# Weighted out-degrees summed by TensorE in the preparation, and a plain copy for the eviction of the adjacency bins

## The reference

```python
deg_out = jax.ops.segment_sum(w, s, num_segments=n)   # s: sources and a loop per node
deg_in = jax.ops.segment_sum(w, d, num_segments=n)
inv_sqrt_out = jnp.where(deg_out > 0, jax.lax.rsqrt(deg_out), 0.0)
wn = w * inv_sqrt_out[s] * inv_sqrt_in[d]
def step(h, _):
    agg = jax.ops.segment_sum(h[s] * wn[:, None], d, num_segments=n)
    return ((1.0 - ALPHA) * agg + ALPHA * feat_0, None)
h, _ = jax.lax.scan(step, feat, None, length=K)       # K = 10
```

## Time and profile before

| | before |
|---|---|
| three runs | 4495.53, 4504.68 and 4504.80 us; median 4504.68 us |
| the profiled execution | 4496.91 us, of which its span is 4495.1 us |
| mean granted TensorE clock | 0.867 |
| busy share of the span | PE 70%, PEld 48%, DVE 61%, ACT 21%, POOL 64% |

### The profile page before, as it was taken

How to read it: one execution, slowest core, us unless ns; L and a number is a source line. 1 busy time by engine, 2 the same in 40 slices (tenths; PEclk the granted TensorE clock), 3 DMA queues, 4 the chain that set the end, 5 groups by cost and what they waited for, 6 DMA issues and landing times.

```text
span 4495.1 us, 80143 instructions
## 1 busy us (share of the span) xinstructions
PE 3133.2 (70%) x19503; PEld 2178.5 (48%) x19514; DVE 2732.8 (61%) x9895; ACT 932.9 (21%) x3282; POOL 2884.3 (64%) x3059
## 2 busy tenths in 40 slices
PE   1240117777777999999788875887858778566665
PEld 1240015555554443444366664666646666445554
DVE  6970228777776111111588877888878888765554
ACT  0000003333332000000122221222213222111211
POOL 2677766545556888870277774777747777467776
PEclk9999959989987999999899997999979999755555
DMA  4310024333338999999422223222232222211112
GB/s 143 112 40 10 17 65 88 78 79 81 83 79 217 363 356 362 355 365 354 156 62 62 63 61 51 62 62 62 62 53 62 62 62 62 38 31 28 28 28 30
DMA packets 296107, 497.96 MB, mean 111 GB/s; under 512 B 166411, under 2 KB 211340, under 8 KB 294474
## 3 DMA queue, kind: packets, MB, share of 16 engines
q1 hardware_dynamic: 120919, 340.03, 21.5%
q0 software_dynamic: 92160, 115.39, 14.0%
q10 hardware_dynamic: 82800, 40.01, 3.1%
HBM read 435.66 MB, written 59.08 MB: 110 GB/s over the span
## 4 chain that ended last, share of the span: by engine, by line
PE 30%; POOL 25%; issue 20%; DMA 13%; DVE 9%; DVEq 1%; ACT 1%; SPq 1%; POOLq 0%; another core or an unknown queue 0%; ACTq 0%
PE ps L1571 27%; POOL arena L827 17%; DMA arena<-table,arena 10%; POOL rows_dst L810 7%; DMA rows_dst<-stage,arena 1%; DVE arena L1174 1%; DVE arena L1173 1%; DMA arena<-in_edge_attr_dram 1%; PE ps L1753 1%; DVE arena L1158 1%; DVEq L554 1%; DVE arena L1192 1%; DVE arena L1345 1%; DVE arena L1188 1%; PE ps L1802 1%
## 5 line engine op out<-in xcount | busy, mean ns | idle before, releaser
L827 POOL DMA_INDIRECT arena<-table,arena x2080 | 1981.9, 953 | 1244.2 <-issue 548.8
L1571 PE MATMUL ps<-arena 128*128 128x96 f32 (+4 forms) x8940 | 1485.3, 345 | 616.9 <-DVE arena L1192 255.6
L1571 PEld LDWEIGHTS ps<-arena 128*128 128x128 f32 (+3 forms) x8940 | 1140.4, 217 | 951.4 <-issue 690.2
L1571 PE MATMUL ps<-arena,nodes 125*64 125x500 f32 (+2 forms) x3144 | 649.4, 537 | 32.8 <-DMA arena<-dense 22.3
L1174 DVE TENSOR_SCALAR arena<-iota_row_b,arena 128x128 f32<-128x128 bf16 x2080 | 581.0, 296 | 0.0
L781 POOL DMA_INDIRECT rows_src<-stage,stage_at x400 | 478.0, 1195 | 117.3 <-issue 110.3
L810 POOL DMA_INDIRECT rows_dst<-stage,arena x400 | 393.1, 983 | 229.0 <-issue 124.1
L1186 DVE TENSOR_TENSOR arena<-ps,arena 128x256 f32<-128x256 f32 x416 | 176.3, 424 | 531.2 <-DMA arena<-table,arena 515.8
L1173 DVE TENSOR_SCALAR arena<-iota_row_b,arena 128x128 bf16<-128x128 bf16 x1664 | 456.4, 276 | 2.6 <-PE ps L1571 0.9
L1571 PEld LDWEIGHTS ps<-arena,nodes 125*64 125x64 f32 (+1 forms) x3144 | 242.8, 137 | 351.9 <-issue 319.4
L1277 DVE TENSOR_TENSOR nodes<-nodes,ps 125x256 f32 (+1 forms) x70 | 27.5, 392 | 607.3 <-PE ps L1753 607.3
(11 more groups left out here) (289 smaller groups left out, 3382.2 us busy)
## 6 DMA issues: line engine op xcount, KB each, us to landing
arena<-dense SPq DMA_DIRECT2D x240, 750.0 KB, 7.2
nodes<-dense SPq DMA_DIRECT2D x60, 750.0 KB, 8.2
dense<-arena ACTq DMA_DIRECT2D x150, 250.0 KB
arena<-table,arena POOLq DMA_INDIRECT x2080
arena<-dense SPq DMA_DIRECT2D x60, 500.0 KB, 7.7
arena<-rows_dst SPq DMA_DIRECT2D x208, 96.0 KB
arena<-dense SPq DMA_DIRECT2D x6, 2000.0 KB, 21.2
arena<-pair_rows SPq DMA_DIRECT2D x12, 976.6 KB
```

The lines of the kernel that those rows point to most:

```text
L827: nc.gpsimd.indirect_dma_start(rows[:, u, k, 0:width], None, frm, bass.IndirectOffsetOnAxis(ap=p[:, c, j, c_other:c_other + 1].bitcast(I32 ...
L1571: return nc.tensor.matmul(to, lhsT, rhs, start=start, stop=stop, skip_group_check=True)
```

## The change

The out-degrees no longer come from the eviction. After `place(1, ...)` DVE makes, for each of the 400 tiles of 125 edges, a one-hot of `lo` of the source (`lo_one`, 125 x 128, a ring of `OR = 5`), and for every 50 tiles (`OC = 50`) the product of the one-hot of `hi` with the edge weights (`src_w`, 125 x 50 x 25, two buffers). TensorE adds up 400 matmuls (125 x 128 weights, 25 columns, 32-bit floats) in bank 6, and DVE copies the sum to `deg[:, 0, :]`. All this stands on DVE's list ahead of the first layer norm, and on PE's list behind the look-ups. The eviction of a group becomes one COPY; `deg_parts` and its reduction go. `src_w` and `lo_one` lie on the room of `dst_one`, which is no longer read by then.

```diff
+OC, OR = 50, 5
             place(1, pos_src[:])
+            v.wait_ge(at_loaded, 16 * 2)
+            for c in range(EJ // OC):
+                js = slice(c * OC, (c + 1) * OC)
+                if c >= 2:
+                    v.wait_ge(out_used, OC * (c - 1))
+                link(nc.vector.tensor_tensor(src_w[:, c % 2], src_one[:, js, :], wgt[:, js].unsqueeze(2).to_broadcast([EP, OC, HI]), ALU.mult))
+                for j in range(c * OC, (c + 1) * OC):
+                    if j >= OR:
+                        v.wait_ge(out_used, j - OR + 1)
+                    nc.vector.tensor_scalar(lo_one[:, j % OR, :], iota_row_b[0:EP, :], lo[:, 0, j:j + 1], None, ALU.is_equal).then_inc(out_ready, 1)
+            v.wait_ge(out_summed, 1)
+            link(nc.vector.tensor_copy(deg[:, 0, :], ps[0:LO, 6, 0:HI]))
             v.wait_ge(loaded, 16 * (len(loads) + len(block_loads)))
             layer_norm(link, xs[:], t1[:], t2[:], 0)
...
-            nc.vector.tensor_reduce(deg[:, 0, :], deg_parts[0:LO].rearrange("p d s -> p s d")[:, 0:HI, :], AX_X, ALU.add)
...
-                for r in range(blocks):
-                    ins = nc.scalar.activation(ev[:, slot, r * LO:(r + 1) * LO], ps[:, bank, r * LO:(r + 1) * LO], ACT.Copy,
-                                               accum_out=deg_parts[:, bass.ds(d, 1), g * CB + r])
-                ins.then_inc(ev_ready, 1)
+                nc.scalar.copy(ev[:, slot, 0:blocks * LO], ps[:, bank, 0:blocks * LO]).then_inc(ev_ready, 1)
...
+            for j in range(EJ):
+                pe.wait_ge(out_ready, j + 1)
+                ins = mm(ps[:, 6, 0:HI], lo_one[:, j % OR, :], src_w[:, j // OC % 2, j % OC, :], start=j == 0, stop=j == EJ - 1)
+                ins.then_inc(out_used if j < EJ - 1 else out_summed, 1)
             pe.wait_ge(w3_ready, 1)
```

More of the change, by code:

```diff
@@ L89 @@
 JR = 8
+OC, OR = 50, 5
+assert EJ % OC == 0
 EP_L0, EP_L2, EP_L3 = 0, 1, 1 + LAYERS
@@ L225, in gnn_kernel @@
         used[0] = WORDS - HI * (CG * CB)
-        deg_parts = carve([128, HI, CG * CB])
         used[0] = 0
@@ L290, in gnn_kernel @@
         at16 = carve([EP, EJ, DA])
+        out_from = used[0]
         dst_one = carve([EP, 2, GC, GP], BF16)
+        out_to = used[0]
+        used[0] = out_from
+        src_w = carve([EP, 2, OC, HI])
+        lo_one = carve([EP, OR, 128])
+        assert used[0] <= out_to
+        used[0] = out_to
         assert used[0] <= KEEP_FROM, (used[0], KEEP_FROM)
@@ L503, in gnn_kernel @@
         built = sem("built")
+        out_ready = sem("out_ready")
+        out_used = sem("out_used")
+        out_summed = sem("out_summed")
         bank_free = sem("bank_free")
```

## The result

| | before | changed |
|---|---|---|
| median | 4495.53 us (5 runs) | 4473.67 us (5 runs) |
| ratio to before, 95% interval | 1 | 0.9941, 0.9919 to 0.9962 |
| the same, repeated beside 11 runs of before | 4497.88 us | 4471.67 us; 0.9944, 0.9932 to 0.9957 |
| the profiled execution's span | 4495.1 us | 4462.0 us |

What follows compares the result with a forecast made beforehand. POOL's sends were taken to bound the preparation, TensorE's and DVE's steps each other in the first layer. Terms 4 - 7 - 1.4 = -4.4 us gave 4500.3 us on the level of the runs' median; range 4487 to 4515 us.

Steps and rivals of the forecast that it cites:

- The loop fits: Preparation: the new loop, 0.43 us a matmul, 172 us, hides in DVE's hole before ACT's root; cost 0 us.
- The first rival: Preparation: matmuls do not overlap, the loop takes 320 us and POOL stands still; 4614 us, chance 0.08.
- What the loop does to POOL: Preparation: DVE's eight products lengthen POOL's sends, comparisons add 0; 4 us lost, bounds 0 and 9.
- The second rival: Preparation: comparisons lock the ports shared with POOL, which loses 19 to 38 us; about 4528 us, chance 0.06.
- The eviction: First layer: banks return 0.64 us earlier, shortening TensorE's 19 waits; 7 us gained, bounds 0 and 12.
- The end of the layer: Between the first layer's last matmul and the second layer: the reduction goes, 1.3 us, plus 0.1 of an accumulator read.
- The third rival: First layer: the whole 12 us of bank waits gained, 3 more from ACT's shorter list, POOL unharmed; 4488 us, chance 0.2.

Runs made afterwards that it cites:

- act_copies: Changed kernel with ACT copying the one-hots of `hi` in place of DVE's products, the comparison multiplying by the weight; 0.9925 of the kernel before.
- evict_only: Kernel before with the new plain-copy eviction but not the new loop, out-degrees set to one; 0.9929 of the kernel before.
- unrolled_before: Kernel before with its evictions written out for all 25 d instead of a loop, so no jump back; 0.9971 of the kernel before.
- act_copies_again: act_copies measured again, beside the changed kernel on one chip; 4464.40 us against 4471.67, 0.9927 of the kernel before.
- copy_twice: Changed kernel with each bank copied twice, so that it returns later, with no accumulator; 0.9986 of the kernel before.
- twice_padded: copy_twice with 31 semaphore increments at two places of each d, lengthening ACT's loop body; 1.0012 of the kernel before.

## Why the prediction was wrong, point by point

*The loop fits.* Right in every number: 0.43 us a matmul (0.43 forecast), weight loads of 333 ns (near 324), the request at 485.15 us (485), and ACT's root 25 us behind it. The first rival did not come.

*What the loop does to POOL.* Right in mechanism, too small: 4 us with bounds 0 and 9. Nine of the 147 sends that begin in the stretch last over 1.2 us. Two of them stand beside the layer norm, like both long ones before; the other seven each meet a product. 57 ns more on the mean make 8.4 us. Over all kernels here, the nine with the products start the first layer at 667.9 us on average, the nine without at 659.0. The forecast took the low end of 4 to 7 us because not every product would meet a send at a bad moment; seven of eight did. The second rival, that the comparisons cost as much, falls: the median send beside them takes 959 ns in the changed kernel (958 before), and `act_copies`, which keeps all 400, has a mean of 981 ns.

The Trainium skill, "SBUF — State Buffer", section "Who interferes with whom", says that a DVE instruction with two inputs in SBUF contends with a GpSimd instruction that reads there. By that rule the eight products stretch sends, and the trace agrees with the seven long sends above; that a tensor_scalar holds up a send for its whole length, no send here shows.

*The eviction: the step that failed.* "Where TensorE waited for it, 19 times, that is at most 19 x 0.64 = 12 us" took a label for a count, and made a bound of it. The term was put at 7 us, and measured 33 in the layer of the profile and 32 in the time of `evict_only`. In its place the runs showed three things:

- There were 34 steps that waited for a bank, 36.3 us, of which 21.9 went (37, 38.4 and 23.3 with the gaps that end at other matmuls). The cut itself was well sized: by the timelines the return takes 1.76 us before (772.21 to 773.97 us) and 1.18 after, 0.58 us less against 0.64. With the right count the same product, 34 x 0.64 = 22 us, gives what these gaps lost, in part by luck, since some of it is the jump's.
- ACT's jump, five times 2.6 to 3.1 us before and 0.2 after, was part of it: 3 to 12 us of the layer (10 in `unrolled_before`, of which 7 are gaps at a step). The prediction counted instructions only as durations, never as the length of a loop's body.
- TensorE's matmuls took 11 to 17 us less, with less time at 1.2 GHz. That this follows from the shorter waits, and what of the layer's 33 us it makes, was not shown apart: the four kernels whose layer takes over 730 us are busy 579 to 581 us in it, and most others 555 to 575, but `act_copies_again` has 578 us with 17 gaps.

Late return (18 to 20 us for 0.47 us in `copy_twice`) and jump (12 us from there to `twice_padded`) give the old layer back, so no cost of the accumulators is left over that one profile could tell (some 5 us).

*The end of the layer.* L1225 is gone; its 1.3 us are too few to be seen in these times.

*The rivals and the range.* The third rival (banks worth more, 4488 us) had the right sign, at 0.2, and was itself held down by the same 12 us. The low end of the range came from it, and so missed. With the terms as measured the sum is 9 - 33 - 1 = -25 us, though the 33 are of one profile each; the two halves by the times of all runs give 11 - 32 = -21 us.

## What to carry to other kernels

A wait with two semaphores is put down to one of them: before a row of waits becomes a bound, look whether the other release always stands the same short time ahead of the gap's end, and count those gaps under any name. Where a change alters how many instructions a loop's body has, look at the time between its branch and the next instruction, before and after; it stands in no row of busy time. An engine that is idle two thirds of a stretch can still be what others wait for, because its work comes in rushes (here the last groups of a `d` in close order, and every fourth `d` a jump).

## What was not expected of the hardware

- The jump back takes ACT 0.2 us where 269 or 297 instructions lie between two branches, and 2.4 to 3.4 us with 429, 541, 545 or 569. The Trainium skill, "Runtime: NRT & Kernel Launch", section "Instruction fetch mechanics", says that a taken branch whose target is not in the current window of two pages stalls for a fetch, and gives most engines room for 512 instructions. The stall is there, and so are fewer fetches (62 packets for 104); but 429 instructions are fewer than 512 and stall too, so for this program the limit lies between 297 and 429. Where in the code the loop begins was not varied, so another program may have another limit.
- One DVE product of 1.46 us lengthens a POOL send that it meets by about 1 us on average (the seven long ones in the loop last 1.3 to 2.2 us, the median of all 0.96); 400 comparisons beside the sends add at most 17 ns to the mean of a send (981 ns in `act_copies`, 964 before).
- In the loop the clock column reads 1.00, while weight loads take 333 ns, about as long as where it reads 0.50 (328 ns), and not the 196 ns of 2400 to 2600 us, where it reads 0.95. By the loads, as in the look-ups, the column does not show the level there.
